# Swapped banks of the gated blocks, x's low part on GpSimd, and an fp16 output projection of the last batch, in an attention and gated feed-forward kernel

## What is computed

```python
x  = L0_attn_x                                   # 4 x 1024 x 256, float32
xn = layernorm(x)
# attention, 16 heads of 16, keys = values
q, kv = rotary(split(xn @ Wq)), rotary(split(xn @ Wkv))
out = softmax((q * SCALE) @ kv^T) @ kv
attn = merge(out) @ Wout + bout
# gated feed-forward, int weights times 1/127, hidden size 768
ffn = (silu(xn @ wg^T) * (xn @ wu^T)) @ wd^T
result = x + attn + ffn
```

## Time and profile before

| | |
|---|---|
| median of 3 runs | 842.49 us (840.6 to 842.92) |
| profiled execution, its own time | 840.95 us |
| its span, first to last instruction | 839.0 us |
| TensorE busy | 796.6 us (95%) |
| VectorE busy | 745.7 us (89%) |
| ScalarE busy | 691.3 us (82%) |
| GpSimd busy | 256.3 us (31%) |
| chunk stage | 0 to 213 us |
| attention loop | 218 to 826 us |

### The profile page before, as it was taken

The page is one execution under the profiler, slowest core; times in us unless marked ns, Lnnn a source line. Parts: engine busy times, 40 slices in busy tenths (PEclk is TensorE's granted clock), DMA queues, the critical chain, the costliest instruction groups (busy, mean ns, idle before and its releaser), DMA issues.

```text
span 839.0 us, 19118 instructions
## 1 busy us (share of the span) xinstructions
PE 796.6 (95%) x7316; PEld 294.6 (35%) x7316; DVE 745.7 (89%) x898; ACT 691.3 (82%) x1268; POOL 256.3 (31%) x490
## 2 busy tenths in 40 slices
PE   4879898889899999999999999999999999999997
PEld 2345454345433332333333333333333333333234
DVE  6988878788799999999999999999999999999702
ACT  4566454543799999999999999999999999999982
POOL 3876766657220000011222222222222222222210
PEclk9999999999999999999999999999999999999999
DMA  9565456444111111112122212221122211221222
GB/s 313 124 142 128 102 123 127 98 91 123 52 29 32 42 35 29 36 30 44 45 53 55 61 48 51 57 56 51 48 55 57 59 49 48 55 58 53 80 70 78
DMA packets 111679, 60.54 MB, mean 72 GB/s; under 512 B 71372, under 2 KB 101900, under 8 KB 111588
## 3 DMA queue, kind: packets, MB, share of 16 engines
q1 hardware_dynamic: 111588, 59.32, 28.2%
HBM read 28.57 MB, written 16.90 MB: 54 GB/s over the span
## 4 chain that ended last, share of the span: by engine, by line
PE 87%; DVE 3%; ACT 3%; issue 1%; POOL 1%; DVEq 0%; ACTq 0%; POOLq 0%
PE ps L750 33%; PE ps L767 18%; PE ps L732 15%; PE ps L626 8%; PE ps L640 4%; ACT arena L1011 2%; PE ps L606 1%; PE ps L607 1%; PE ps L608 1%; PE ps L675 1%; PE ps L778 1%; DVE side L1121 1%; DVE negmax L1176 1%; DVE stats L1053 1%; PE ps L794 1%
## 5 line engine op out<-in xcount | busy, mean ns | idle before, releaser
L1176 DVE TENSOR_REDUCE negmax<-ps 128x2 f32<-128x1024 f32 x512 | 588.7, 1211 | 6.9 <-PE ps L767 6.4
L1011 ACT ACTIVATE arena<-ps 128x512 f32<-128x512 f32 x1024 | 555.4, 595 | 32.4 <-PE ps L732 10.6
L750 PE MATMUL ps<-arena 128*32 128x256 f32 x4072 | 326.5, 392 | 2.4 <-issue 2.2
L732 PE MATMUL ps<-qs,ks 51*128 51x512 f16 x1024 | 197.9, 382 | 3.3 <-ACT arena L1011 2.1
L767 PE MATMUL ps<-ks,qs 48*128 48x512 f16 x972 | 189.4, 386 | 0.0
L750 PEld LDWEIGHTS ps<-arena 128*32 128x32 f32 x4072 | 80.4, 107 | 128.1 <-issue 127.0
L767 PEld LDWEIGHTS ps<-ks,qs 48*128 48x128 f16 x972 | 46.5, 92 | 195.1 <-DVE negmax L1176 138.6
L626 PE MATMUL ps<-arena,side 128*128 128x512 f16 x384 | 89.0, 380 | 4.3 <-DVE side L1121 4.3
L1428 POOL TENSOR_TENSOR arena<-arena,x_all 128x256 f32<-128x256 f32 x22 | 16.0, 728 | 229.5 <-ACT arena L1032 229.5
L732 PEld LDWEIGHTS ps<-qs,ks 51*128 51x128 f16 x1024 | 50.6, 92 | 77.8 <-ACT arena L1011 45.9
L1361 POOL TENSOR_TENSOR mparts<-rowmax,munit 128x16 f16<-128x16 f32 x32 | 7.5, 236 | 210.5 <-DVE rowmax L1186 210.5
(11 more groups left out here) (115 smaller groups left out, 512.2 us busy)
## 6 DMA issues: line engine op xcount, KB each, us to landing
parts_d<-arena SPq DMA_DIRECT2D x64, 128.0 KB
x_all<-x_dram SPq DMA_DIRECT2D x8, 512.0 KB, 9.0
qs<-parts_d SPq DMA_DIRECT2D x64, 64.0 KB, 1.9
ks<-parts_d SPq DMA_DIRECT2D x64, 64.0 KB, 1.9
o_d<-arena SPq DMA_DIRECT2D x124, 32.0 KB
arena<-o_d SPq DMA_DIRECT2D x24, 128.0 KB
arena<-inv_d SPq DMA_DIRECT2D x48, 64.0 KB
out_dram<-arena SPq DMA_DIRECT2D x24, 128.0 KB, 1.8
```

Source lines behind the costliest of these rows:

```text
L732: mm = pe.matmul(ps[:, score_bank(place(p, kt, 2 * half + a)), :], ks[ring][top:top + ROWS, kt * P:(kt + 1) * P], qs[ring][top:top + ROWS, ...
L750: mm = pe.matmul(ps[32 * j:32 * j + 32, 7, cols], vstage[pl % 2][:, j % 2, kt, :], probs[PER_STEP * (kt % PBUF) + j][:, cols], start=(kt = ...
L1011: act.activation(probs[PER_STEP * (kt % PBUF) + j], ps[:, score_bank(place(p, kt, j)), :], ACT.Exp).then_inc(exp_done, 1)
L1176: dve.tensor_reduce(negmax[pl % 2][:, h, :, kt], ps[:, bank:bank + 2, :], AX.X, ALU.max, negate=True).then_inc(max_done, 1)
```

## The change

- `GATE_BANKS` is turned round: even blocks in banks 0 and 1, odd ones in 6 and 7. Block 0 waits for the rotation of tiles 0 and 1, block 1 for the previous chunk's last block; `project` waits for one block less.
- `low_x` leaves VectorE for GpSimd, as two subtractions, between `keep_values` and the first `low_hid`. In chunk 1 the moments are spread over more places.
- Tiles 21 and 23 are the late ones now, at slot 13 of pair 30 and slot 10 of pair 31; tile 22 goes the common way in slot 3 of pair 31. All are split on GpSimd.
- The last batch's rows are divided and split into fp16 parts on VectorE (`osplit`, in the place of the reciprocals). Each projection is three fp16 matmuls; the eight of the front are spread over pairs 30 and 31. `wlast` is scaled once more on GpSimd, and the last additions multiply by `wo_unit` and take two tiles each.
- The last eight matmuls alternate between tiles 0 to 3 (rows 0 to 63) and 4 to 7 (rows 64 to 127).

```diff
-LATE_AT = {6: 22, 11: 23}
-FRONT_AT = {0: 2, 1: 3, 2: 4, 4: 5, 7: 6, 8: 7, 13: 0, 14: 1}
-GATE_BANKS = (6, 0)
+LATE_TILES = (PAIRS - LAG - 1, PAIRS - LAG + 1)
+LATE_AT = {(PAIRS - 2, 13): LATE_TILES[0], (PAIRS - 1, 10): LATE_TILES[1]}
+LATE_BANK = 3
+FRONT_AT = {(PAIRS - 2, 10): 0, (PAIRS - 2, 11): 1, (PAIRS - 2, 15): 2, (PAIRS - 1, 1): 3, (PAIRS - 1, 6): 4,
+            (PAIRS - 1, 8): 5, (PAIRS - 1, 12): 6, (PAIRS - 1, 13): 7}
+LAST_ORDER = [t for n in range(CT) for t in (n, n + CT)]
+PAIR_ORDER = [0, 2, 1, 3]
+GATE_BANKS = (0, 6)
...
             def project(c):
...
                     if c and t == 0:
-                        pe.wait_ge(silu_done, KH * c)
-                        pe.wait_ge(hid_done, KH * c)
+                        pe.wait_ge(silu_done, KH * c - 1)
+                        pe.wait_ge(hid_done, KH * c - 1)
...
             def gate_up(c, j):
...
+                if j == 0:
+                    pe.wait_ge(rope_read, CT * c + 2)
                 elif j == 1:
-                    pe.wait_ge(rope_read, CT * c + 2)
-                elif j:
+                    pe.wait_ge(silu_done, KH * c)
+                    pe.wait_ge(hid_done, KH * c)
+                else:
...
-                for j in range(2, KH):
-                    if c + 1 < NCHUNK and j == 2:
-                        low_x(c + 1)
...
                 keep_values(c)
+                if c + 1 < NCHUNK:
+                    low_x(c + 1)
                 for j in range(KH):
                     low_hid(c, j)
...
+            def low_x(c):
+
+                if c == 1:
+                    pool.wait_ge(wud_ready, 2)
+                else:
+                    pool.wait_ge(x_turned, 32 * (c - 1))
+                pool.wait_ge(x_hi_done, c)
+                for k in range(KD):
+                    ins = pool.tensor_tensor(x_lo[:, k, :, :], xn[:, :, k * P:(k + 1) * P], x_hi[:, k, :, :], ALU.subtract)
+                ins.then_inc(x_lo_done, 1)
...
+            def project_last(t, g, rows):
+
+                tok = slice(t % CT * P, (t % CT + 1) * P)
+                for part, w in ((0, wo_hi), (0, wo_lo), (1, wo_hi)):
+                    pe.matmul(last_out(t), osplit[t // CT][0:rows, g, part, tok], w[0:rows, g, :],
+                              start=(g + part == 0 and w is wo_hi and t % 2 == 0), stop=False)
...
-            pe.wait_ge(back_divided, CPB)
+            pe.wait_ge(back_split, 2 * CPB)
...
-            for t in range(BT):
+            for t in LAST_ORDER:
```

More of the change, by code:

```diff
@@ L210, in build @@
         olast = [carve(HG * CHUNK, F32, "p (g n) -> p g n", side, g=HG) for _ in range(2)]
-        ilast = [carve(HG * CHUNK, F32, "p (g n) -> p g n", side, g=HG) for _ in range(2)]
+        ilast_room = [carve(HG * CHUNK, F32, None, side) for _ in range(2)]
+        ilast = [r.rearrange("p (g n) -> p g n", g=HG) for r in ilast_room]
+        osplit = [r.bitcast(FP16).rearrange("p (g s n) -> p g s n", g=HG, s=2) for r in ilast_room]
         rlast = carve(BT * DIM, F32, "p (t d) -> p t d", side, t=BT)
@@ L508, in load_last, with load_last_inv @@
                     sp.dma_start(olast[k][0:rows, g, :], o_d[BATCH - 1, g, 0:rows, tok]).then_inc(landed, 16)
+            def load_last_inv(g, landed):
+                rows = P if g == 0 else BACK_ROWS
+                for k in range(CPB):
+                    tok = slice(k * CHUNK, (k + 1) * CHUNK)
                     src = inv_groups[BATCH - 1, g, 0:rows // DH, tok]
@@ L1251, in pairs_before, with divide_last, add_late @@
                 return (p - slot % 2) // 2 + 1
+            def divide_last(g, landed, done, split):
+                rows = P if g == 0 else BACK_ROWS
+                dve.wait_ge(landed, 16 * 2 * CPB)
+                for k in range(CPB):
+                    dve.tensor_tensor(olast[k][0:rows, g, :], olast[k][0:rows, g, :], ilast[k][0:rows, g, :], ALU.mult
+                                      ).then_inc(done, 1)
+                for k in range(CPB):
+                    hi, lo = osplit[k][0:rows, g, 0, :], osplit[k][0:rows, g, 1, :]
+                    dve.wait_ge(done, k + 1)
+                    dve.tensor_copy(hi, olast[k][0:rows, g, :]).then_inc(split, 1)
+                for k in range(CPB):
+                    hi, lo = osplit[k][0:rows, g, 0, :], osplit[k][0:rows, g, 1, :]
+                    dve.wait_ge(split, k + 1)
+                    dve.tensor_tensor(lo, olast[k][0:rows, g, :], hi, ALU.subtract).then_inc(split, 1)
+            def add_late(n):
+                dve.wait_ge(wout_done, CREDIT + n + 1)
+                dve.wait_ge(res_free[n % 2], 16 * (n // 2))
+                dve.scalar_tensor_tensor(res[n % 2], ps[:, LATE_BANK, 0:DIM], wo_unit[:, 0:1], x_all[:, n, :],
+                                         ALU.mult, ALU.add).then_inc(late_done, 1)
             def step(turn, ls, last_turn=False):
@@ L1435, in slot @@
                 for tile in tiles:
-                    if not isinstance(tile[0], int) or tile[0] < LOOP_TILES:
-                        add_tile(*tile, tile[0])
+                    add_tile(*tile, tile[0])
                 q = j + 1
@@ L1455, in _ @@
                     slot(i + TILES_FROM, FIRST_SLOT + j, [(i * RING + j, j % 2)])
-            for j in range(FIRST_SLOT, RING):
-                n = LAST - LAG + j - FIRST_SLOT
-                slot(TURNS, j, [(n, n % 2)])
-            for n in range(LOOP_TILES, (BATCH - 1) * BT):
+            slot(TURNS, FIRST_SLOT, [(LAST - LAG, (LAST - LAG) % 2)])
+            for n in range(LAST - LAG + 1, (BATCH - 1) * BT):
                 divide(n, n % 2)
+            n = tile_in_pair(PAIRS - 1)
+            add_tile(n, n % 2, n)
 def rotary_tables():
```

145 lines of the change are left out of this document (64 added, 81 removed).

## The result

The changed kernel takes **834.66 us** (median of six runs, 830.85 to 836.11); the kernel before, timed beside it, 841.89 us (840.60 to 842.92). The profiled execution took 833.6 us, its span 831.8.

The account below looks back on a forecast made before the run. TensorE was taken as the bound (87% of the chain, full clock), with its or ScalarE's waits to gain. Chunk stage 12.7 us plus tail 3.6 gave -16.3: 824.7 from 840.95, 826.2 from the median; 825.5 taken, range 821 to 832.

Parts of the forecast that it names:

- The stage: Chunk stage, 0 to 213 us: removing TensorE's waits before leads and projections was to gain 12.7 us.
- the tail: Last two pairs and behind the loop, 782 us on: -3.4 + 0.7 + 0.7 - 1.6 = -3.6 us.
- part 2: Chunk stage, low_x on GpSimd: hidden there, gains 1.64 us in each of chunks 3 to 6, 0.9 in chunk 2.
- part 6: Last batch's back rows: reciprocal loads queue late on SP, so the back projections wait, costing 0.7 us.
- Part 1: Chunk boundaries: swapped gated banks free the projection, gaining 0.93 us at each of five boundaries after chunks 2 to 6.
- Part 3: Chunks 0 and 1: low_x delays `down` to about 42.5 us, absorbed by the next wait; chunk 2's second block 0.6 us earlier.
- Part 4: Front projections in pairs 30 and 31: three fp16 passes each cut ScalarE's waits from 5.5 to 2.1 us, gaining 3.4.
- Part 5: Pair 31, slot 10: tile 23's division, now three operations, is ready too late, costing 0.7 us.
- Part 7: Behind the loop: shorter back projections gain 1.3 us, wider additions 0.3, alternating row halves nothing; sum -1.6 us.
- A: Rival, chunk stage: removing one wait shows the next, each of four chunks gains only 1.3 us; 830.6 us, 14%.
- B: Rival, tail gives nothing: tile 23 and the back rows each cost 2.5 us through DRAM round trips; 829.1 us, 8%.

Follow-up runs that it names:

- e6: Kernel before with only the gated blocks' banks swapped, low_x still on VectorE; 834.28 us, ratio 0.9904.
- e3: Changed kernel with dummy matmuls both before the first lead of chunk 2 and before the first back projection; 831.64 us, ratio 0.9864.
- e12: Changed kernel with no lead in chunk 2 and SyncE's 16 reloads moved behind the transposes of chunk 3's x and chunk 2's q and k; 828.89 us.
- e13: Changed kernel with leads from chunk 3, later reloads, tail loads and stores reordered, tile 21's store earlier, back rows split by halves; 826.76 us, ratio 0.9818.
- e14: Changed kernel unaltered, profiled a second time; 832.79 us, ratio 0.9895.
- e15: Changed kernel unaltered, profiled a third time; 832.73 us, ratio 0.9897.
- e1: Changed kernel with 18 dummy matmuls before the first lead of chunk 2; 832.25 us, ratio 0.9867.
- e2: Changed kernel with 8 dummy matmuls before the first back projection; 832.59 us, ratio 0.9867.
- e4: Changed kernel with low_x of chunks 1 and 2 back on VectorE, GpSimd keeping it from chunk 3 on; 830.65 us, ratio 0.9858.
- e8: Changed kernel with no lead in chunk 2 and five in each of chunks 3 to 6; 833.31 us, ratio 0.9905.
- e9: Changed kernel with tile 23's loads ahead of pair 30's output stores, and inverse sums' stores ahead of the back rows' loads; 831.61 us, ratio 0.9873.
- e10: Changed kernel with the back rows divided and split by halves of tokens, TensorE first waiting for one half only; 831.33 us, ratio 0.9870.
- e5: Kernel before with the chunk stage's half alone: swapped banks and low_x on GpSimd; 832.55 us, ratio 0.9887.
- e7: Changed kernel with the last eight matmuls, additions and stores in plain order instead of alternating row halves; 832.80 us, ratio 0.9890.

## Why the prediction was wrong

The forecast was 825.5 us (821 to 832); the kernel takes 834.66. The stage was to give 12.7 us and gave 8.7 in the profiled execution; the tail was to give 3.6 and cost 1.5. Two steps failed: part 2 called the move of `low_x` hidden in chunk 2, and part 6 priced the back wait at 0.7 us; and no term of the sum was a half clock. Part by part:

- **Part 1, the swapped banks: right** in mechanism, a little small: 1.09 us a boundary (e6), not 0.93. After chunk 0 it gave nothing: the projection starts at 35.41 us as before, after a wait of 1.16 us. The profile names no releaser, but VectorE's `low_w`, which the projection needs too, ends 0.2 us earlier (at 35.20), and so it does in e3, e12, e13, e14 and e15, where that projection starts anywhere from 34.39 to 37.29 us.
- **Part 2, `low_x` on GpSimd: right for chunks 3 to 6** (1.72 us a chunk, forecast 1.64; 2.27 us for two operations, 2.4 forecast), **wrong for chunk 2**, and this is the first step that failed. It read "Queued behind it are six `low_hid`", and followed GpSimd's queue, but not who waits for `low_x` itself: the transpose on SyncE, and behind that the stores, the 16 reloads and the first lead. Projection 3 was to start 2.4 us earlier; it started 2.5 us later (89.24 against 86.72). The 4.9 us of miss at this point is the lead's wait, 4.25 us, and 2.1 us of half clock behind it (e1), less 1.2 us by which TensorE came to the lead earlier than thought in that execution and 0.3 us by which the stretch behind it is shorter than thought at full clock. Chunks 3 to 6 then gave 1.0 us more than forecast, so the stage is 4.0 short. Part 1 did say "The work thus brought forward must find its inputs", looked at the transposes and `hl`, and left out the one input that goes through DRAM.
- Of the Trainium skill's advice in "GPSIMD Engine Reference", section 4.1, the trace shows both sides. GpSimd's 2.27 us are 1.2 to 1.9 times VectorE's 1.21 to 1.91 for the same data, up to the factor of about two; they are hidden in chunks 3 to 6, and on the path, by way of SyncE's queue, in chunk 1.
- **Part 3, chunks 0 and 1:** `down` at 41.94 us (forecast 42.5), in the other executions with `low_x` on GpSimd there 41.83 to 43.81; the delay did die in the next wait (1.67 us instead of 2.33, and the block behind it starts at 52.47 instead of 52.27). In size it lies within the scatter.
- **Part 4, front projections: mis-sized.** ScalarE's waits came to 3.7 us, not 2.1. A front slot cost it 0.17 to 0.30 us where 0.12 was worked out, tile 21's slot 0.63 instead of 0.45, and tile 23's 0.95 instead of 0.45, of which 0.39 is the wait of part 5.
- **Part 5, tile 23:** division done at 806.87 us, asked for at 806.62: 0.39 us of wait, forecast 0.7.
- **Part 6, the back rows: the second step that failed.** The loads were issued when forecast (at 808.22 us, 8.7 before the 816.9 of the forecast, as the whole stage), but the two took 5.8 us (808.22 to 813.98) where I had put 4.1: wait 1.76 us instead of 0.7. What made it dear is what no part had: the clock fell behind the wait, 3.1 us (e2). The text priced the wait at its own length and no more.
- **Part 7, behind the loop:** with the clock full the projections and sums take 4.65 us against 5.75 of before, 1.1 less, near the 1.3 forecast. For the row halves I took no gain against the rule of the Trainium skill, "TensorEngine Tiling (Array Packing)", "Key Properties". The trace agrees with the rule: 2.96 us become 2.00. For the time my choice was nonetheless nearer (0.13 us), but by luck: VectorE's additions end last, not TensorE's weight loads. (They take 0.74 us each, not 0.6, so the 0.3 us forecast for them is 0.13 with the alternation. Half of 2.96 is 1.5 us, where the text gave 1.2.)
- **The rivals:** A (each removed wait shows the next, SyncE's queue among them) had the right engine but the wrong place; B had both round trips of the tail, priced at 829.1, and one of them, tile 23's, cost 0.39 us only. It was part of each at once, and neither contained a clock. The clock "at full speed throughout" in the trace of before was taken for granted for the trace after.

Shown by runs: the lead's wait and its clock (e1, e12), the late queue behind it (e4), the place of the 16 reloads in SyncE's order (e8, e12), the back wait and its clock (e2, e9, e10), the worth of the two parts of the stage (e5, e6), the worthlessness of the tail's half as it stands (e5). Mended, the tail's half does give something: the last stretch is 624.8 us in e10 without a fall of the clock, and 624.8 in e13 with 1.7 us of one, against 626.5. Open is why SyncE's four stores took 3.1 and 2.9 us instead of 1.9 in e1 and e3, and what decides, at the same wait, whether the clock falls.

## What to carry to other kernels

When an engine's wait is removed, list every DMA that the consumers ahead will ask for, and its slack in the old trace; one that landed just in time is the next wait, all the more if its producer is moved to a slower engine. Follow a moved operation through every in-order queue behind it, SyncE's too: the order of issue there (reloads behind the transposes) was worth 3.1 us (e12 against e8), nearly what the tail's whole half of the change was meant to bring. Where a wait of TensorE is let stand, look in the trace at the granted clock behind it: here the half clock cost half of what the lead's wait did, on top of it, and nearly twice the length of the back wait. A wait that cost no clock in one execution can cost it in the next.

## What the runs showed of the hardware

- **The clock behind a wait.** Before its lead wait of 3.6 to 4.9 us TensorE had been busy at 2.4 GHz; in all of the nine profiles that had it unfilled on the changed kernel's code or its stage's half, the granted clock fell to 0.5 (1.2 GHz), for some 3 to 7 us: from the lead to projection 3 they took 10.0 to 11.4 us, against 8.5 with the wait filled. Before the back wait of 1.76 to 2.31 us it had done narrow value passes. Seven profiles had such a wait: the clock was at half at once or within 1 us in three (changed, e12, e14: 7.5 to 7.9 us to the last eight), fell later in three (e4, e8, e15: 6.2 to 6.3), and held in one (e7, 4.65), at 2.00 us of wait. Waits of 1.17 us (e9) and 0.59 (e10), and all those of before, up to 2.33 us, cost no clock. But the same waits of the chunk stage, with fp16 passes at 2.4 GHz ahead of them, did cost it in other profiles: those of 2.30 to 2.34 us in chunk 1 in 7 of 17 cases, the 1.65 us at the last lead in 3 of 17. Tile 23's waits of 1.94 and 2.02 us did both times (e3, e1), the 2.88 us of e8 did not. Once the kernel was under way, no fall came behind a wait of 1.5 us or less. Dummy matmuls in the wait kept it up each time (e1, e2, e3).
- **Row halves.** Sixteen fp32 passes of 64 rows take 0.185 us each in plain order and 0.125 alternating between the two halves of rows.
- **SyncE's queue.** A load of the reload takes 0.44 us to issue, so sixteen hold up for 7.3 us (73.44 to 80.73) whatever stands behind them; in e12 they took 9.5 us.
